# Four triangle layers on one core: gate tiles loaded during the triangle stage, last residuals behind the first T tiles, layer 0's variance of whole squares, layer 3's high part read in place

## What is computed

```python
xn   = layernorm(gn(x)) * w + b              # layers 0 to 2; layer 3 takes gn(x) itself
left = (xn @ Wl) * sigmoid(xn @ Wlg) * mask  # right alike; biases in layers 1, 2; no mask in 2
gate = sigmoid(xn @ Wog)
T    = einsum('bikd,bjkd->bijd', left, right)       # layers 0, 1 (layer 0 in bf16)
T    = einsum('bkjd,bkid->bijd', left, right)       # layers 2 (divided by 192) and 3
# layers 0, 2:  (layernorm(T) * gate) @ Wout
# layers 1, 3:  (layernorm(T) @ Wout) * gate
```

## Time and profile before

| | us |
|---|---|
| three runs | 1522.71, 1524.15 (median), 1531.39 |
| the profiled execution | 1531.67 |
| its span in the trace | 1529.5 |
| busy: TensorE (PE) | 1282.1 (84%) |
| busy: VectorE (DVE) | 1041.8 (68%) |
| busy: ScalarE (ACT) | 962.0 (63%) |
| busy: GpSimd (POOL) | 543.4 (36%) |

### The profile page before, as it was taken

The page is one execution under the profiler, slowest core; times in us unless marked ns, Lnnn a source line. Parts: engine busy times, 40 slices in busy tenths (PEclk is TensorE's granted clock), DMA queues, the critical chain, the costliest instruction groups (busy, mean ns, idle before and its releaser), DMA issues. The chain is left out here.

```text
span 1529.5 us, 43851 instructions
## 1 busy us (share of the span) xinstructions
PE 1282.1 (84%) x12950; PEld 765.9 (50%) x12950; DVE 1041.8 (68%) x2976; ACT 962.0 (63%) x2093; POOL 543.4 (36%) x490
## 2 busy tenths in 40 slices
PE   0899998787789998989941999999789677799898
PEld 0455554444345455755521666667455333367455
DVE  7577774299789996219950788831499788821587
ACT  0577774489577774129940888831599688822575
POOL 0455551055456563005530666610156200000355
PEclk9899999899899999999975899999899899999999
DMA  8011113467533332896667333359689444369798
GB/s 275 27 52 46 51 51 111 114 202 225 169 101 103 106 115 72 254 286 177 195 152 188 103 115 113 108 174 300 180 262 278 154 141 138 129 185 307 212 291 258
DMA packets 206501, 249.31 MB, mean 163 GB/s; under 512 B 29024, under 2 KB 196320, under 8 KB 206432
## 3 DMA queue, kind: packets, MB, share of 16 engines
q1 hardware_dynamic: 206432, 248.42, 53.1%
HBM read 139.83 MB, written 108.53 MB: 162 GB/s over the span
## 5 line engine op out<-in xcount | busy, mean ns | idle before, releaser
L989 DVE SCALAR_TENSOR_TENSOR lr<-ps,mask,act_out 128x128 f32 (+5 forms) x1152 | 276.3, 310 | 61.7 <-ACT act_out L739 55.6
L1153 POOL TENSOR_TENSOR rstd<-ve,half_col 128x6 f32<-128x6 f32 x144 | 190.2, 1321 | 259.1 <-DVE ve L962 225.4
L511 PE MATMUL ps<-w_parts,val 64*128 64x256 bf16 (+1 forms) x2112 | 222.6, 304 | 47.4 <-DVE lr L989 41.9
L1196 POOL TENSOR_TENSOR new_ring<-val,lr 128x384 f32<-128x384 f32 x96 | 103.4, 1078 | 409.5 <-issue 325.0
L1186 POOL TENSOR_TENSOR val<-act_out,gate_ring 128x384 f32<-128x384 f32 x96 | 118.4, 1233 | 247.2 <-ACT act_out L817 231.1
L739 ACT ACTIVATE act_out<-ps 128x384 f32<-128x384 f32 x384 | 174.9, 481 | 34.2 <-PE ps L511 16.7
L783 ACT ACTIVATE in_ring<-ps 128x768 f32<-128x768 f32 (+1 forms) x64 | 51.8, 810 | 184.0 <-PE ps L579 161.9
L511 PEld LDWEIGHTS ps<-w_parts,val 64*128 64x128 bf16 (+1 forms) x2112 | 90.5, 111 | 133.3 <-DVE lr L989 94.7
L1085 DVE TENSOR_TENSOR sq_low<-sq 128x384 bf16<-128x384 f32 x192 | 120.1, 625 | 52.9 <-ACT sq L796 52.8
L621 PE MATMUL ps<-in_ring,k 128*128 128x384 f32 x288 | 134.5, 555 | 20.1 <-DMA in_ring<-t_scratch 19.7
L715 ACT ACTIVATE cen<-ps,gn 128x384 f32<-128x384 f32 x144 | 83.6, 581 | 104.1 <-PE ps L466 101.5
(11 more groups left out here) (101 smaller groups left out, 2574.8 us busy)
## 6 DMA issues: line engine op xcount, KB each, us to landing
gate_scratch<-gate_ring SPq DMA_DIRECT2D x192, 192.0 KB, 2.2
gate_ring<-gate_scratch SPq DMA_DIRECT2D x96, 384.0 KB, 3.7
in_ring<-x_scratch SPq DMA_DIRECT2D x144, 192.0 KB, 2.4
lr<-x_scratch SPq DMA_DIRECT2D x72, 384.0 KB, 4.5
in_ring<-t_scratch SPq DMA_DIRECT2D x144, 192.0 KB, 3.3
x_scratch<-new_ring SPq DMA_DIRECT2D x48, 384.0 KB, 2.9
t_scratch<-in_ring SPq DMA_DIRECT2D x48, 384.0 KB, 3.4
lr<-x SPq DMA_DIRECT2D x6, 1536.0 KB, 15.3
```

The costliest lines, as they stand in the source:

```text
L511: mm = nc.tensor.matmul(banks[h][:, :, 0:P], moving(x, s)[half(h), N * r:N * r + P], proj_weights(w, h)[:, 0:2 * P], start=start, stop=sto ...
L989: ins = nc.vector.scalar_tensor_tensor(out5[:, h, lo // 2:hi // 2, :, m], ps[:, 4 + 2 * r + h, lo:hi].rearrange("p (a e) -> p a e", e=2), ...
L1153: nc.gpsimd.tensor_tensor(rstd[:, s % 2, :], ve[:, s % 2, :], half_col[:, :], ALU.pow)\
```

## The change

Four edits, cut to their core:

```diff
+LATE = 14
+        xn_high = xn[:, :, :].bitcast(BF16).rearrange("p s (f e) -> p s f e", e=2)[:, :, :, 1]
+        def residual_count(l, late):
+            return 16 * sum(len(freed_slots(m, g)) for m in range(1, l + 1) for g in range(GROUPS) if (g >= LATE) == late)
# SP, phase_b1, after a group's planes
-                    for n in freed_slots(l, g) if l else []:
-                        sp.dma_start(slots[...], two_tiles(x_src(l), n)).then_inc(res_loaded, 16)
+                    for n in freed_slots(l, g) if l and g < LATE else []:
+                        load_residual(l, n, res_loaded)
+                    if g == LATE - 2:
+                        for s in range(RING):
+                            sp.wait_ge(gate_stored[s], (l + 1) * 16 * TURNS)
+                        for n in range(0, RING, 2):
+                            load_gate(l, n, n)
# SP, phase_b2, head
                 for n in range(0, RING, 2):
                     load_t(n, n)
-                    load_gate(n, n)
+                for g in range(LATE, GROUPS) if l else []:
+                    for n in freed_slots(l, g):
+                        load_residual(l, n, late_loaded)
# PE, phase_a, moving()
+                    if not ln and part == 0:
+                        return xn_high[:, s % 2, :]
# PE, phase_b2, variance()
+                    if l == 0:
+                        pe.wait_ge(b2_sq, base + n + 1)
+                        for j in range(CHUNKS):
+                            mm = nc.tensor.matmul(ps[:, 6 + s % 2, 2 * j:2 * j + 2],
+                                                  sq[:, s % 2, P * j:P * j + P], k_sel, start=True, stop=True)
+                        mm.then_inc(b2_var, 1)
+                        return
# PE, phase_b2, head
-                for n in range(4):
-                    centre(n, 0, n)
+                centre(0, 0, 0)
+                centre(1, 0, 1)
                 keep_clock(4, 1)
                 variance(0, 0)
-                keep_clock(4, 1)
+                centre(2, 0, 2)
                 variance(1, 1)
                 spread(0, 0)
-                keep_clock(4, 1)
-                centre(4, 1, 0)
+                centre(3, 0, 3)
                 spread(1, 1)
                 variance(2, 2)
+                centre(4, 1, 0)
# ACT, phase_a: plain() and the step
-                    slot_free(act, a_lo, parts_before(l) + n - 1)
+                    slot_free(act, a_proj, l * SUBS + ROWS * (n - 1))
                     gate(n, i, s)
-                    if not ln and ahead >= 1:
-                        high(n + 1, (s + 1) % RING)
-                    if not ln and ahead >= 2:
-                        plain(n + 2, i + (s + 2) // RING, (s + 2) % RING)
...
                     sigmoids(n, s, 0)
                     sigmoids(n, s, 1)
+                    if not ln and ahead >= 2:
+                        plain(n + 2, i + (s + 2) // RING, (s + 2) % RING)
# DVE, phase_a, low(), for layer 3
+                        dve.wait_ge(a_xn, base + n + 1)
+                        slot_free(dve, a_proj, l * SUBS + ROWS * (n - 1))
+                        nc.vector.tensor_tensor(xn_parts[:, s % 2, 1, :], xn[:, s % 2, :], xn_high[:, s % 2, :],
+                                                ALU.subtract).then_inc(a_lo, 1)
# DVE, phase_b2: square_low only in layers 1 to 3; waits for residuals
-                    dve.wait_ge(res_loaded, 16 * TILES // 2 * l)
+                    dve.wait_ge(res_loaded, residual_count(l, False))
# DVE finish() and POOL residual(), at tile 3 of layers 1 to 3
+                            dve.wait_ge(late_loaded, residual_count(l, True))
```

46 lines of the change are left out of this document (26 added, 20 removed).

## The result

| | before | after |
|---|---|---|
| runs on the same chip | 1522.71 to 1531.39, median 1525.41 (4) | 1500.77 to 1509.64, median 1506.46 (4) |
| the profiled execution, its span | 1531.67, 1529.5 | 1509.19, 1507.0 |
| ratio | | 0.9866, 95% interval 0.982 to 0.9912 |

The changed kernel is faster by 19 us by the medians, 1.3% by the ratio (0.9% to 1.8%). The forecast was 36 us, to 1488 us; the time lies at the upper edge of the range, 1474 to 1508.

The account below looks back on a forecast made before the run. Bounds by stretch: VectorE in layer 0's last stage, VectorE and ScalarE in layer 3's projection, TensorE and DMA busy in its last stage. Gains 9 + 14 + 5 + 4.5 + 3.5 + 0 = 36 us; 1524.15 - 36 = 1488, range 1474 to 1508.

Parts of the forecast that it names:

- Layer 0's term of 9 us: Layer 0's last stage: whole squares free VectorE of sq_low, 2.22 to 2.03 us per tile, 9 us gained.
- Layer 3's term of 14 us: Layer 3's projection stage: high part in place, 2.79 to 2.50 us per tile plus 0.5 us, 14 us gained.
- (b): Rival, layer 0's last stage: f32 loads not overlapped, 0.186 us each, 8 us lost, total 1505 us; chance 0.08.
- (c): Rival, layer 3's projection stage: sigmoids remain late or strided operand slow, 2.79 us per tile stays, 1502 us; chance 0.08.
- (d): Rival, layer 0's last stage: f32 passes at 0.30 us or more at lower clock, slower overall, 1548 at 0.34; chance 0.03.
- (a): Rival: the heads give nothing, T(4) and T(6) come behind late residuals, 13 us less, 1501 us; chance 0.10.
- the heads of layers 1 to 3, 13 us forecast: Start of the last stages: out(0) sooner through reordered loads and matmuls, 4.5, 5 and 3.5 us in layers 1 to 3.
- The first centre "2.4 us sooner": Layer 3's head: planes land 0.7 us sooner and T(0) takes 3.2 us instead of 4.9, so centre(0) comes 2.4 us sooner.
- The 2.0 us given back: Layer 3's head: centre(2), centre(3) and centre(4) now stand between variance(0) and out(0), costing about 2.0 us.
- The announced sign: Heads: the prediction is wrong if TensorE waits for T at centre(4) by over 2 us.
- layer 0's head and triangle stage, summed to 0: Layer 0: early gate loads cost about 1.5 us, variance(0) comes about 1.5 us sooner; sum 0, from -2.5 to +1.5.
- the prediction's own sign of being wrong, over 2 us: Layer 1's triangle stage: the prediction is wrong if this stage grows by over 2 us.

Follow-up runs that it names:

- e8: The kernel before with only layer 0's variance taken from whole f32 squares; median 1516.71 us, ratio 0.9945.
- e7: The kernel before with only layer 3's high part read in place; median 1515.11 us, ratio 0.9931.
- e11: The kernel before with only the late residual pairs moved behind T(0), T(2) and the head's gate tiles; median 1530.38 us, ratio 1.0004.
- e2: The changed kernel with TensorE's old head order, four centres and then variance(0); median 1504.81 us, ratio 0.9864 to the kernel before.
- e5: e3 with the late residual pairs behind T(4) and T(6) instead of behind T(2); median 1499.24 us, ratio 0.9836 to the kernel before.
- e3: The changed kernel with centre(3) ahead of spread(0), centre(4) ahead of spread(1), a keep_clock pair between; median 1500.72 us, ratio 0.9826 to the kernel before.
- e1: The changed kernel with the gate loads back in the head behind T(2), all layers; median 1501.85 us, ratio 0.9848 to the kernel before.
- e10: The kernel before with only the gate loads moved to group 12 of the triangle stage; median 1531.42 us, ratio 1.0018.
- e6: e5 with layer 0's gate loads back at the head of its last stage; median 1495.13 us, ratio 0.9805 to the kernel before.

## Why the prediction was right and where it was wrong

**Right: the sign, the range and the two steady stages.** Layer 0's term of 9 us measured 10.6 in the changed kernel and 10.5 in e8 (102.6 to 92.1). The pitch of an f32 pass, taken as 0.11 us from the nearest row, is 0.097. The estimate of 0.64 us for six loads, worked out from the figure of the Trainium skill (page "TensorE: Matmul & The Clock Gate", section "LDWEIGHTS (loading the stationary operand)"), is close to the 0.58 measured at full clock. The sentence of the Trainium skill, same page, section "The mechanism", that weight loads overlap running matmuls only where row groups differ does not describe these passes: without overlap 6 x 0.191 would be 1.15 us. TensorE is the bound as foreseen, VectorE 0.83 busy where below 0.8 was named. Layer 3's term of 14 us measured 11.6, and 11.8 in e7: 2.56 us per tile, not 2.50, and VectorE 0.94 busy, not over 0.95. The mis-sized piece is the products, taken as 1.89 us from the last tiles and 1.99 in the steady stage. Rivals (b), (c) and (d) are refuted for the steady stages.

That the whole lies in the range, by 1.5 us, is luck in part. The likeliest case with the bounds of its terms ended at 1498; the range reached to 1508 for the sake of rivals (a) to (c), and none of them is what happened. The two steady terms erred by 1.6 us one way and 2.4 the other, and some 4 us of the profiles' difference stand in layer 2, where the change does nothing.

**Wrong: the heads of layers 1 to 3, 13 us forecast and 5.8 measured, with 2.2 us of it lost in the triangle stages.** The steps of that sum one by one, on layer 3. The first centre "2.4 us sooner" was 0.9 (9.26 to 8.33 us behind the last plane copy). The planes did not land 0.7 us sooner: that step is right for the late residuals by themselves (0.9 us in e11), but the change's own early gate loads take it back, which the sum did not count. And T(0) needed 3.9 us from issue to the centre, not 3.2. From the first centre to variance(0), 4.4 us sooner, is right: 7.05 to 2.56 is 4.5, of which the order gives 1.5 (e2). The 2.0 us given back were 3.2 (4.25 to 7.46; in layer 1 4.1, in layer 2 1.9). The step counted the three centres that move behind variance(0) and not the place where they meet ScalarE's queue: spread(1) waits for rb(1) behind the copy and square of centre(3), and TensorE, idle twice for 1.4 us, drops to its lower clock, where centre(4) and out(0) take 1.63 and 1.49 us for 0.81 and 0.89. e2 shows that the order of the head is worth nothing in these layers, and e5 that an order with shorter waits (0.65 us for rb) and no lower clock takes 4.8 and 5.2 us off the heads of layers 3 and 1, once T(4) stands ahead of the late residuals. How much is the waits' and how much the clock's was not separated.

**Wrong in its reason: rival (a), the late residuals.** Its mechanism is there, but not as the limit of this kernel. In the changed kernel centre(4) waits for T(4) by 0.61 us in layer 1 and not at all in layers 2 and 3, and that only because spread(0) and spread(1) make centre(4) late. When TensorE has less ahead of centre(4) (e3) it waits 1.92 and 2.05 us in layers 1 and 3, and e5 takes both waits away. The announced sign, a wait over 2 us at centre(4), is thus absent from the changed kernel and appears one edit later.

**Wrong: layer 0's head and triangle stage, summed to 0, measured 5.0 us lost.** The 1.5 us for the two gate loads at group 12 are 3.3 us, in e1 as in e10. The sum had 1.2 us for SP's two issues and 0.3 for contention. The issues are about right: the planes of group 13 are issued 1.4 us later than in e1. The contention is the step that failed: behind 0.8 MB of gate tiles these planes take 4.1 us to land and not 2.0, and ScalarE waits for them, 3.98 us after 0.90. The same edit costs 1.8 us in layer 1's triangle stage, which the forecast had at nothing. There the prediction's own sign of being wrong, over 2 us, did appear: the profile of the changed kernel has 2.5 us more. In layer 0's head variance(0) came 1.7 us sooner, as forecast, but later f32 passes ran at the lower clock: the earlier trace rows has 0.98 for the middle of the stage, and the head is not the middle. Rival (d) named that price (0.25 to 0.34 us per pass) for the wrong stretch; measured there it is 0.19 to 0.20 us to the next start (303.52 to 304.66 for six in the changed kernel, 2.42 us for twelve in e8), for some passes only, and in e8 the head is 2.9 us longer.

So 22.2 us of a forecast of 23 came from the steady stages, and of the 13 from the heads 5.8 came, less 7.2 for the triangle stages and layer 0's head.

## What to carry to other kernels

A term for a steady loop can be read off the round of the engine that binds next, and it came within 2.5 us twice here. A term for a head cannot be read off one chain: lay down the queues of both engines and of the DMAs event by event, since what is moved behind the first product meets the second, and two short waits in a row can cost the clock as well. A load that is moved to another stage has two prices, its issue and what its bytes do to the transfers behind it, if somebody waits for these; here two loads cost 1.4 us by their issue, and the stores behind them took 2 us longer to land, together about the 3.3 us that the stage grew by. Two edits that touch the same queue are not priced one by one: here one took back what the other gave.

## What was not expected of the hardware

Six f32 passes over full-row weights with two columns each follow each other every 0.097 us, at 0.191 us for the load alone, and twice as far apart at the lower clock (1.14 us for six in the changed kernel). The two T loads of 192 KB that e3 issues behind three residual pairs in layer 3 take 4.3 and 6.2 us to land, where the median of the same loads is 3.3 us. The granted clock in one head was 1.00, 0.62 and 0.50 in stretches of 3 us that follow 1.40 and 1.37 us of idle TensorE, and 1.00 from 286 us on in e6's head of layer 0, where TensorE idles 0.76 and 1.27 us, 4.4 us apart, with keep_clock matmuls behind each.
